# Expert routing of one transformer layer: the search for the eight highest logits moved into the LayerNorm stage, the weights onto GpSimd, and the ranks computed ahead of the totals

## The chip, the cores and the metric

One core of a Trainium2 chip runs the whole program. The metric is the device time of one execution in microseconds; the median of three runs of the kernel before is 1215.02 us. A core has five engines, each with its own queue of instructions: TensorE (PE in the profile; its weight loads are PEld), VectorE (DVE), ScalarE (ACT), GpSimd (POOL) and SyncE (SP), which here only starts transfers.

## What is computed

The input is 4 sequences of 512 rows of 512 numbers, 2048 rows in all, in 32-bit floats. The reference, cut to what matters:

```python
x = x + _layernorm(attention(_layernorm(x)))          # 16 heads, causal, rotary
x = x + _layernorm(ffn(_layernorm(x)))
# ffn, for all T = 2048 rows xt:
logits = xt @ router_w.T                              # 64 experts
top_w, top_i = jax.lax.top_k(softmax(logits), 8)
top_w = top_w / jnp.sum(top_w, axis=-1, keepdims=True)
# every row goes to its 8 experts, with these weights:
h_e = (silu(xt @ Wg[e].T) * (xt @ Wu[e].T)) @ Wd[e].T
# and one shared expert takes all rows, scaled by sigmoid(xt @ Wse.T)
```

As the weights are divided by their sum, the softmax over all 64 logits isn't needed in full: exp(logit - highest) of the eight chosen, divided by the sum of those eight, is the same.

## The kernel before

The rows are 16 tiles of 128. The work runs in stages: attention; then the LayerNorm stage; then routing together with the shared expert; then the routed experts, 128 gathered rows at a time; then the last sums and LayerNorm. The order on each engine is written out by hand: every engine's program is a list of operations with waits on semaphores, and an engine does them in that order.

**LayerNorm stage** (a loop over tiles on each engine, staggered). For tile i PE projects the attention's output into PSUM (`project`, L753). DVE takes its statistics (L1048, L1049), ACT the square root (L546), DVE the reciprocal (L1057) and the normalized row `delta` (L1058). POOL adds it to x (L397). In the next turn of the loop DVE takes the statistics of the sum (L1052, L1053), ACT the root (L550), DVE the reciprocal (L1063) and the normalized row `xn` (L1067). SP writes `xn` to memory (L312), for the gathers later, and PE turns it (`turn_x2`, L761); ACT takes it out of PSUM (L557), PE multiplies it by the router (`route`, L769), and ACT takes out 64 logits and the shared expert's one (L562). PE's order in a turn is `project(i)`, `route(i-3)`, `turn_x2(i-2)`.

**Routing**, on DVE unless it is said otherwise, begins when all 16 tiles have logits: the highest (L1072), ACT's Exp (L566), the softmax (L1085), the eight highest of each tile (L1087), their places (L1091, L1094), a running sum over tiles of who chose which expert (L1096, 16 in a chain), the weights (L1101 to L1104) and their transfer by SP (L315). PE counts the rows of each expert (`count_rows`, L814); DVE rounds the counts to tiles of 128 (L1111 to L1115). PE sums those over experts (L821, L822) and computes where each row stands within its expert (`place_rows`): for each half of the tiles, two products of 512 columns (L827, L828) and eight of 64 (L830), accumulated in one bank. DVE turns the places into slot numbers (L1129, then a max for each tile at L1136, then integers). PE's `tile_rows` (L835) and DVE's L1151 to L1158 make the list of which expert each block of 128 slots belongs to. Last, a table from slots to rows: 128 pairs of DVE operations (L1164, L1165) make one-hot matrices in a ring of eight, and PE multiplies each pair into the table (`fill_table`, L841, eight pairs to a tile).

**The shared expert** runs on PE, ACT and POOL at the same time, tile by tile: `shared_up` (L789), ACT's Silu and a copy (L575, L576), POOL's product (L404), `shared_turn` (L799), ACT (L580), `shared_down` (L805), ACT (L584). The routing's PE work is placed in this loop by hand: `count_rows` in the turn i = 3, `place_rows` and `tile_rows` in the turn i = 4, `fill_table(i - 6)` from the turn 6 on, and the last six tiles of it behind the loop. Behind its products POOL writes the shared rows to memory (L408, two transfers of 2 MB), and SP loads the weights of one more expert (L317).

**The routed stage** begins with DVE's L1169 to L1183 behind the last L841, the first gather by POOL (L414) and `turn_rows` (L870).

## Time and profile before

| what | us |
|---|---|
| median of 3 runs (1214.99 to 1217.04) | 1215.02 |
| the profiled execution's own time | 1215.08 |
| its span, from first to last instruction | 1213.2 |
| PE busy | 1055.3 (87%) |
| DVE busy | 702.6 (58%) |
| POOL busy | 628.7 (52%) |
| ACT busy | 469.4 (39%) |
| mean granted TensorE clock | 0.943 |

The times of the sections below are microseconds from the span's start in that one profiled execution. Its own time is 1.9 us over its span. "x8" behind an operation is the number of instructions merged into a row; a 32-bit product is two records. The bracket at the end of a row is the engine's idle time before it and what ended it. Ends of matmuls are modelled, and busy shares are means over a stretch.

### The profile page before, as it was taken

To read this page: it belongs to the slowest core of one execution; us is meant where nothing else is said; L and a number is where in the kernel's file an instruction comes from. 1 tells how busy PE (TensorE), PEld (TensorE's weight loads), DVE (VectorE), ACT (ScalarE), POOL (GpSimd) and SP (SyncE) were. 2 spreads that over 40 slices of the span, in tenths; PEclk is the share of its full clock that TensorE was granted. 3 is DMA by queue.
4 is the path that set the end of the run, shared out by engine and by line. 5 is a ranking of instruction groups with operands and counts; after the bars stand their busy time and mean duration, and the time that the engine had idled before them with its cause. 6 is when DMAs were issued, how large, how long until landed. Compare 5 with 4: busy or idle time off the path is not lost.

```text
span 1213.2 us, 24246 instructions
## 1 busy us (share of the span) xinstructions
PE 1055.3 (87%) x6243; PEld 717.2 (59%) x6244; DVE 702.6 (58%) x2355; ACT 469.4 (39%) x1354; POOL 628.7 (52%) x633
## 2 busy tenths in 40 slices
PE   5799899899999989878879999999999999999300
PEld 3455566555666545546447777777777777777200
DVE  3666566556666668758845544545444544454287
ACT  1666566556666732242212222222222222222122
POOL 4333333333333312200138888888888888788534
PEclk9899999989999999889969999999999999999755
DMA  9600000000000061100339999999999999997592
GB/s 353 230 2 1 4 1 2 3 2 2 1 2 2 1 234 52 61 18 1 115 117 210 221 212 256 227 240 239 264 228 256 230 255 265 253 201 136 118 386 98
DMA packets 65968, 166.80 MB, mean 137 GB/s; under 512 B 15570, under 2 KB 16850, under 8 KB 65760
## 3 DMA queue, kind: packets, MB, share of 16 engines
q0 software_dynamic: 38816, 83.95, 31.3%
q1 hardware_dynamic: 27072, 81.88, 19.2%
q8 instruction: 38, 0.62, 0.2%
q14 instruction: 42, 0.34, 0.1%
HBM read 121.03 MB, written 62.65 MB: 151 GB/s over the span
## 4 chain that ended last, share of the span: by engine, by line
PE 69%; DMA 11%; DVE 10%; issue 4%; ACT 2%; POOL 2%; DVEq 0%; POOLq 0%; SPq 0%; ACTq 0%
PE ps L886 16%; PE ps L638 14%; PE ps L897 8%; DMA sum_rows<-x_t,idx 6%; PE ps L697 6%; PE ps L753 4%; PE ps L870 4%; PE ps L667 4%; PE ps L717 4%; DMA x_t<-x_rows,idx 3%; PE ps L789 2%; PE ps L652 2%; POOL sum_rows L420 1%; PE ps L769 1%; PE ps L805 1%
## 5 line engine op out<-in xcount | busy, mean ns | idle before, releaser
L886 PE MATMUL ps<-big,work 128*128 x1264 | 300.8, 381 | 0.0
L420 POOL DMA_INDIRECT sum_rows<-x_t,idx x157 | 250.1, 1593 | 51.1 <-issue 41.1
L886 PEld LDWEIGHTS ps<-big,work 128*128 128x128 f32 x1264 | 229.0, 191 | 24.9
L414 POOL DMA_INDIRECT x_t<-x_rows,idx x163 | 170.5, 1046 | 71.5 <-issue 30.8
L638 PE MATMUL ps<-big 128*128 128x384 f32 x512 | 180.5, 496 | 1.5 <-ACT big L483 1.1
L359 POOL TENSOR_TENSOR work<-qkv_all,rope_sb 128x256 f32<-128x256 f32 x64 | 46.7, 730 | 251.6 <-ACT qkv_all L488 251.5
L594 ACT ACTIVATE work<-ps 128x512 f32<-128x512 f32 x159 | 95.0, 597 | 198.4 <-PE ps L870 147.9
L897 PE MATMUL ps<-big,work 128*128 x314 | 161.1, 594 | 0.9 <-issue 0.7
L870 PEld LDWEIGHTS ps<-ident_sb,x_t 128*128 128x128 f32 x636 | 79.0, 143 | 101.9 <-issue 75.9
L970 DVE CUSTOM_DVE_ANT_0 ps<-ps,mask_sb 128x128 f32<-128x128 f32 (+3 forms) x256 | 120.8, 512 | 24.0 <-PE ps L667 23.4
L505 ACT ACTIVATE work<-ps,neg_max 128x128 f32<-128x128 f32 (+3 forms) x256 | 132.4, 528 | 4.3 <-DVE neg_max L970 3.2
L638 PEld LDWEIGHTS ps<-big 128*128 128x128 f32 x512 | 94.5, 195 | 56.4 <-issue 3.7
L1198 DVE SCALAR_TENSOR_TENSOR work<-work,small,ps 128x128 f32<-128x128 f32 x157 | 54.5, 347 | 123.6 <-ACT work L599 92.5
L599 ACT ACTIVATE work<-ps 128x128 f32<-128x128 f32 x157 | 43.6, 278 | 196.3 <-PE ps L886 140.5
L697 PE MATMUL ps<-ident_sb,work 128*128 128x128 f32 x640 | 98.9, 285 | 18.2 <-ACT work L505 10.5
L511 ACT ACTIVATE x_t<-ps 128x128 f32<-128x128 f32 (+2 forms) x192 | 77.1, 436 | 91.7 <-PE ps L697 91.7
L870 PE MATMUL ps<-ident_sb,x_t 128*128 128x128 f32 x636 | 97.5, 276 | 14.3 <-DMA x_t<-x_rows,idx 12.5
L1206 DVE TENSOR_SCALAR x_t<-ps 128x512 f32<-128x512 f32 x157 | 106.9, 681 | 0.0
L697 PEld LDWEIGHTS ps<-ident_sb,work 128*128 128x128 f32 x640 | 69.0, 141 | 55.1 <-issue 44.4
L991 DVE TENSOR_TENSOR attn_t<-ps,work 128x128 f32 (+1 forms) x64 | 18.7, 292 | 112.3 <-PE ps L717 112.3
L1192 DVE TENSOR_SCALAR small<-x_t 128x1 f32 x158 | 24.3, 154 | 81.0 <-issue 77.3
L897 PEld LDWEIGHTS ps<-big,work 128*128 128x128 f32 x314 | 59.0, 190 | 11.4 <-issue 3.7
(166 smaller groups left out, 1419.4 us busy)
## 6 DMA issues: line engine op xcount, KB each, us to landing
big<-experts SPq DMA_DIRECT2D x65, 768.0 KB, 14.7
sum_rows<-x_t POOLq DMA_DIRECT2D x4, 2048.0 KB
big<-sum_rows SPq DMA_DIRECT2D x6, 1024.0 KB, 11.0
x_sb<-x SPq DMA_DIRECT2D x4, 1024.0 KB, 15.2
x_rows<-work SPq DMA_DIRECT2D x16, 256.0 KB, 2.0
sum_rows<-attn_t POOLq DMA_DIRECT2D x2, 2048.0 KB
out<-x_sb SPq DMA_DIRECT2D x16, 256.0 KB, 2.1
x_t<-sum_rows SPq DMA_DIRECT2D x3, 1024.0 KB, 14.5
```

The costliest lines, as they stand in the source:

```text
L414: pool.indirect_dma_start(rows[:, q, :], None, x2_rows, bass.IndirectOffsetOnAxis(ap=idx[:, q, 0:1], axis=0), bounds_check=last_row, oob_i ...
L420: pool.indirect_dma_start(sum_rows[p], bass.IndirectOffsetOnAxis(ap=idx[:, q, 1:2], axis=0), y_sb[:, q, :], None, bounds_check=last_row, o ...
L505: act.activation(probs[:, h, 0:n], s_bank[h][:, 0:n], ACT.Exp, bias=neg_max[:, h:h + 1], scale=-1.0, accum_out=den[:, h:h + 1]).then_inc(s ...
L511: act.activation(probs_t[:, i % 2, h, 0:qt + 1, :], pt_bank[h % 2].rearrange("p (k n) -> p k n", k=TB)[:, 0:qt + 1, :], ACT.Copy).then_inc ...
L594: act.activation(rows_t[:, p, :, :], ps[:, p, :].rearrange("p (c n) -> p c n", c=DC), ACT.Copy).then_inc(s_xg, 1)
L638: mm = pe.matmul(bank[:, 0:QKV], x_t[:, c, bass.ts(t, P)], wqkv_sb[:, c, g % G, :], start=(c == 0), stop=(c == DC - 1))
L697: mm = pe.transpose(pt_bank[h % 2][:, bass.ts(c, P)], probs[:, h, bass.ts(c, P)], ident_sb[:, :])
L870: mm = pe.transpose(ps[:, p, bass.ts(c, P)], rows[:, q, bass.ts(c, P)], ident_sb[:, :])
L886: mm = pe.matmul(ps[:, 2 + p, 0:GATEUP], rows_t[:, p, c, :], w_ring[:, slot, c * GATEUP:(c + 1) * GATEUP], start=(c == 0), stop=(c == DC - 1))
L897: pe.matmul(ps[:, 5 + p, :], hidden_t[:, p, :], w_ring[:, slot, DC * GATEUP:WCOLS], start=True, stop=True).then_inc(s_dn, 1)
L970: dve.tensor_tensor_reduce(sc, sc, mask_sb[:, S - n:S], -SCALE, 3.0e38, ALU.add, ALU.min, neg_max[:, h:h + 1]).then_inc(s_masked, 1)
L1206: dve.tensor_scalar(y_sb[:, q, :], ps[:, 5 + q % 2, :], 1.0, None, ALU.mult).then_inc(s_y, 1)
```

## The change

In the LayerNorm stage DVE does, for the tile whose logits are there (k = i - 4), a max of eight (`top`), a match_replace into `unchosen` and a comparison that gives `chosen`. `xn` is no longer computed by DVE: DVE makes -mean x 1/std in a small column, and ACT computes `xn` with it. POOL adds up `earlier` tile by tile behind L397, for the tile k = i - 4. ACT exponentiates the difference from the highest logit, for the eight highest and for all 64, in one operation each. POOL multiplies the weights by `chosen` and by 1/sum, between its products of the shared expert. On PE the two products of a half that need no totals (`spread_rows`) are done ahead of and behind `count_rows`, all in turn 0 of the shared loop, and the eight products of 64 columns of a half are one of 512. `tile_rows` moves to turn 2, `fill_table(i - 4)` begins in turn 4, and four tiles of it are left behind the loop.

```diff
+        unchosen = work[:, 384:512].rearrange("p (a e) -> p a e", a=2)
+        top_e = work[:, 512:512 + TILES * K].rearrange("p (t k) -> p t k", k=K)
...
@@ gpsimd
-            for i in range(TILES):
-                pool.wait_ge(s_stat, i + 1)
-                pool.tensor_tensor(out=x_sb[:, i, :], in0=x_sb[:, i, :], in1=delta[:, i % 2, :],
-                                   op=ALU.add).then_inc(s_x1, 1)
+            for i in range(TILES + 4):
+                if i < TILES:
+                    pool.wait_ge(s_stat, i + 1)
+                    pool.tensor_tensor(out=x_sb[:, i, :], in0=x_sb[:, i, :], in1=delta[:, i % 2, :],
+                                       op=ALU.add).then_inc(s_x1, 1)
...
+                if i >= 4:
+                    k = i - 4
+                    pool.wait_ge(s_chosen, k + 1)
...
+                    pool.tensor_tensor(out=earlier[:, k + 1, :], in0=earlier[:, k, :], in1=chosen[:, k, :],
+                                       op=ALU.add).then_inc(s_prefix, 1)
...
+                if i == 1:
+                    pool.wait_ge(s_e1, 1)
+                    pool.tensor_tensor(out=prob_e, in0=prob_e, in1=chosen, op=ALU.mult).then_inc(s_masked_e, 1)
+                if i == 3:
+                    pool.wait_ge(s_share, 1)
+                    pool.wait_ge(s_masked_e, 1)
+                    share = rt[:, 3, :].rearrange("p (t o) -> p t o", o=1).broadcast_to([P, TILES, E])
+                    pool.tensor_tensor(out=prob_e, in0=prob_e, in1=share, op=ALU.mult).then_inc(s_comb, 1)
@@ scalar
+                if 1 <= i <= TILES:
+                    r = i - 1
+                    act.wait_ge(s_nmr, r + 1)
+                    if r >= 2:
+                        act.wait_ge(s_x2d[r % 2], 16 * (r // 2))
+                        act.wait_ge(s_x2t_ps, r - 1)
+                    act.activation(xn[:, r % 2, :], x_sb[:, r, :], ACT.Identity, bias=small[:, r % 4, 7:8],
+                                   scale=small[:, r % 4, 6:7]).then_inc(s_x2, 1)
+
+            act.wait_ge(s_log, TILES)
+            act.activation(rt[:, 4, :], logits[:, :, E], ACT.Exp, scale=-1.0).then_inc(s_e2, 1)
             act.wait_ge(s_neg, 1)
-            for i in range(TILES):
-                act.activation(prob_e[:, i, :], logits[:, i, 0:E], ACT.Exp, bias=rt[:, 0, i:i + 1],
-                               accum_out=rt[:, 1, i:i + 1]).then_inc(s_e1, 1)
-            act.activation(rt[:, 4, :], logits[:, :, E], ACT.Exp, scale=-1.0).then_inc(s_e1, 1)
+            act.activation(top_e, top_e, ACT.Exp).then_inc(s_e2, 1)
+            act.wait_ge(s_neg, 2)
+            act.activation(prob_e, prob_e, ACT.Exp).then_inc(s_e1, 1)
@@ tensor
+            def spread_rows(half):
...
+                pe.wait_ge(s_prefix, 8 * half + 8)
...
+                pe.matmul(o, before_sb[:, :], mine, start=True, stop=False)
+                pe.matmul(o, ones_sb[:, :], ahead, start=False, stop=False)
...
-                    pe.matmul(o, before_sb[:, :], mine, start=True, stop=False)
-                    pe.matmul(o, ones_sb[:, :], ahead, start=False, stop=False)
-                    for k in range(8):
-                        mm = pe.matmul(o[:, k * E:(k + 1) * E], n_rep, below_sb[:, :], start=False, stop=(k == 7))
-                mm.then_inc(s_slots_ps, 1)
+                    below_8 = below_sb[:, :].rearrange("f (o e) -> f o e", o=1).broadcast_to([E, 8, E])
+                    pe.matmul(ps[:, half, :], n_rep, below_8, start=False, stop=True).then_inc(s_slots_ps, 1)
...
-                if i == 4:
+                if i == 0:
+                    spread_rows(0)
+                    count_rows()
+                    spread_rows(1)
                     place_rows()
                 if i >= 1:
                     shared_turn(i - 1)
-                if i == 4:
+                if i == 2:
                     tile_rows()
                 if i >= 1:
                     shared_down(i - 1)
-                if i == 3:
-                    count_rows()
-                if i >= 6 and i < TILES:
-                    fill_table(i - 6)
-            for n in range(TILES - 6, TILES):
+                if i >= 4 and i < TILES:
+                    fill_table(i - 4)
+            for n in range(TILES - 4, TILES):
                 fill_table(n)
@@ vector, LayerNorm stage
+            for i in range(TILES + 4):
+                y_in, x_in, l_in = i < TILES, 1 <= i <= TILES, i >= 4
+                r, k = i - 1, i - 4
...
+                if l_in:
+                    dve.wait_ge(s_log, k + 1)
+                    tops = mark(dve.max(top[:, k, :], logits[:, k, 0:E]))
...
+                if l_in:
+                    dve.wait_ge(s_own, tops)
+                    left = mark(dve.match_replace(unchosen[:, k % 2, :], top[:, k, :], logits[:, k, 0:E], MASKED))
...
+                if l_in:
+                    dve.wait_ge(s_own, left)
+                    dve.tensor_scalar(chosen[:, k, :], unchosen[:, k % 2, :], MASKED, None, ALU.is_equal).then_inc(s_chosen, 1)
...
-                    dve.tensor_scalar(xn[:, r % 2, :], x_sb[:, r, :], small_x[:, 4:5], small_x[:, 6:7],
-                                      ALU.subtract, ALU.mult).then_inc(s_x2, 1)
-            dve.wait_ge(s_log, TILES)
...
+                    dve.scalar_tensor_tensor(out=small_x[:, 7:8], in0=small_x[:, 4:5], scalar=-1.0, in1=small_x[:, 6:7],
+                                             op0=ALU.mult, op1=ALU.mult).then_inc(s_nmr, 1)
+
+            def highest(n):
+                return top[:, :, 0:1].broadcast_to([P, TILES, n])
+
+            dve.tensor_tensor(out=top_e, in0=top[:, :, :], in1=highest(K), op=ALU.subtract).then_inc(s_neg, 1)
+            dve.tensor_tensor(out=prob_e, in0=logits[:, :, 0:E], in1=highest(E), op=ALU.subtract).then_inc(s_neg, 1)
```

Left out here: L1072 to L1104 are removed from DVE; behind L1115 it takes the sum of the eight exponentials and the two reciprocals (of that sum and for the sigmoid); and L1129 waits for each half by itself.

## Rows read from the trace of the kernel before

**Rows 1.** Busy us (count) by engine and stretch, PEclk, DMA share, GB/s:

```profile
450.00:470.00 20.00, 20.00 (x84) 11.70 (x83) 16.40 (x37) 5.65 (x19) 5.10 (x5) 1.00 0.20 75
...
510.00:517.00 7.00, 5.63 (x24) 4.73 (x24) 0.89 (x4) 2.08 (x7) 0.00 (x0) 0.50 0.20 75
...
540.00:560.00 20.00, 18.22 (x88) 11.99 (x88) 12.24 (x64) 3.57 (x10) 0.93 (x2) 1.00 0.12 28
```

**Rows 2.** Timeline, one LayerNorm tile: start us, us, engine, line, operation [idle before]:

```profile
495.57 0.70 DVE L1048 BATCH_NORM_STATS2 stats<-ps 128x6 f32<-128x512 f32 x1 [0.47 <-PE ps L753]
...
497.37 0.81 DVE L1058 TENSOR_SCALAR work<-ps,small 128x512 f32<-128x512 f32 x1
...
498.26 1.26 POOL L397 TENSOR_TENSOR x_sb<-x_sb,work 128x512 f32<-128x512 f32 x1 [3.45 <-DVE work L1058]
...
498.29 1.52 DVE L1067 TENSOR_SCALAR work<-x_sb,small 128x512 f32<-128x512 f32 x1
...
500.29 0.70 DVE L1048 BATCH_NORM_STATS2 stats<-ps 128x6 f32<-128x512 f32 x1 [0.47 <-PE ps L753]
...
500.81 0.48 PEld L761 LDWEIGHTS ps<-ident_sb,work 128*128 128x128 f32 x4
```

**Rows 3.** Lines L1067, L617, L1237, L468: ns minimum/median/maximum, first and last start:

```profile
L1067 DVE TENSOR_SCALAR work<-x_sb,small x16: 546/1522/1525, 442.7 to 510.6; 128x512 f32<-128x512 f32 x16
...
L617 ACT ACTIVATE big<-big,moments,rstd x8: 799/801/814, 1166.4 to 1181.3; 128x512 f32<-128x512 f32 x8
...
L1237 DVE TENSOR_TENSOR big<-big x8: 683/686/1752, 1156.3 to 1171.0; 128x512 f32<-128x512 f32 x8
...
L468 POOL TENSOR_TENSOR x_sb<-x_sb,big x8: 1515/1707/1708, 1167.3 to 1184.9; 128x512 f32<-128x512 f32 x8
```

**Rows 4.** Timeline, start and end of the LayerNorm stage on PE:

```profile
444.27 0.66 PE L761 MATMUL ps<-ident_sb,work 128*128 128x128 f32 x4 [0.90 <-DVE work L1067]
...
516.39 5.19 PE L789 MATMUL ps<-big,x_t 128*128 128x256 f32 x16
...
526.23 0.46 PE L799 MATMUL ps<-ident_sb,work 128*128 128x128 f32 x1 [4.65 <-POOL work L404]
```

**Rows 5.** Timeline, the stretch of the ranks:

```profile
539.29 0.14 DVE L1111 COPY n_col<-ps 64x1 f32<-64x1 f32 x1
...
540.59 0.24 PE L821 MATMUL ps<-n_col,upto_sb 64*64 64x1 f32 x2 [1.87 <-DVE qkv_all L1115]
...
540.96 1.12 PE L827 MATMUL ps<-qkv_all,before_sb 128*128 128x512 f32 x2
...
542.88 2.00 PE L830 MATMUL ps<-below_sb,qkv_all 64*128 64x64 f32 x16
...
548.90 0.48 PE L835 MATMUL ps<-qkv_all,ones_sb 64*1 64x192 f32 x2
```

**Rows 6.** Timeline of DVE, slots and first pairs:

```profile
550.07 2.12 DVE L1136 MAX8 work<-wo_sb 128x8 f32<-128x64 f32 x16
...
554.47 0.24 DVE L1164 TENSOR_SCALAR low<-count_h,work 128x128 f16<-128x128 f16 x1
...
554.87 0.23 DVE L1164 TENSOR_SCALAR low<-count_h,work 128x128 f16<-128x128 f16 x1
```

**Rows 7.** Timeline, groups of L841 and their end:

```profile
553.86 1.89 PE L789 MATMUL ps<-big,x_t 128*128 128x256 f32 x8
...
557.41 0.94 PE L841 MATMUL ps<-high,low 128*128 128x192 f16 x8
...
595.75 0.82 PE L841 MATMUL ps<-high,low 128*128 128x192 f16 x8
...
616.10 0.36 DVE L1169 COPY qkv_all<-ps 128x192 f32<-128x192 f32 x1 [0.43 <-PE ps L841]
```

**Rows 8.** A stretch of two us behind the loop, and the first gather:

```profile
610.00:612.00 2.00, 1.69 (x6) 0.52 (x5) 2.00 (x12) 0.00 (x0) 0.00 (x0) 0.50 0.10 39
...
618.67 1.09 POOL L414 DMA_INDIRECT x_t<-x_rows,idx  x1 [18.57 <-DVE idx L1183]
```

## What the change will do: the prediction

> **What bounds the kernel now.** The profiled execution takes 1215.08 us (span 1213.2), 0.06 over the 1215.02 median of the runs, so its sums hold for the median as well. A measurement of this kernel can tell about 0.2% (2.4 us) from no change. The diff touches only 433 to 618 us; I read the busy time of that stretch first, then its timeline tile by tile.
>
> In the LayerNorm stage PE is busy 20.00 of 20 us, and a tile takes 4.72 us from one L1048 to the next [rows 1, 2]. DVE is busy 16.40 of 20, so it has room. The search for the eight highest begins on all tiles at once, behind the last logits, which leave PE about when L789 starts (516.39). PE still does L789 for two tiles and then has nothing: L799 at 526.23 had 4.65 us of idle time ahead of it [rows 4]. The ranks then hold PE's queue from L821 at 540.59 to L835 behind the last L830 at 548.90, 8.3 us [rows 5], and only at 554.47 does DVE begin the 128 pairs of L1164 and L1165 [rows 6]. Their matmuls (L841, eight to a tile) start at 557.41 and are issued once per tile of the shared expert, every (595.75 - 557.41)/9 = 4.26 us: PE bound. The six groups left over at 595.75 go at DVE's pace, 0.40 us a pair, and end at 616.10 [rows 6, 7]. That end releases the first gather at 618.67, and everything behind it is the routed stage, which the change doesn't touch. So the path that counts is: LayerNorm tiles, ranks, ten groups at PE's pace, six at DVE's. What moves 616.10 moves the end.
>
> **LayerNorm stage.** Removed from DVE: L1067, 1.52 us at the median though 0.55 when nothing is in its way [rows 3]. It starts 0.03 us after POOL's L397 (498.29 against 498.26) and is held by it: its end, 1.55 after POOL's start, less its own 0.55 gives a release 1.00 us after POOL's start [rows 2, 3]. ACT does this work instead, in the form of L617, 0.80 us [rows 3]. DVE gains a max, a match_replace, an is_equal and a one-column product. The max of 16 tiles ends within 2.12 us, 0.13 each [rows 6]; match_replace and is_equal on 64 columns have no row here that I use, so between nothing and L1048's 0.70 each; I take 0.2, near the small max. DVE drops in sum, so it hides them. What counts is where they stand: between L1048 and L1058 they add about 0.15 (max and match_replace mostly run while DVE would wait for its own statistics), and by as much L1058 and POOL's L397 start later.
>
> The new product (into small column 7) stands where L1067 stood, 0.03 us behind the start of L397, and reads two SBUF operands. Nearest rows: L1237, two SBUF operands, takes 0.68 alone and 1.75 beside POOL [rows 3]; L1067 is held 0.98. Bounds: held not at all, or for POOL's whole 1.27. I take 1.00, then 0.16 of its own, 0.06 to hand over and 0.80 on ACT: the normalized row is there 2.02 us after POOL's start, where L1067 had it at 1.55. The Trainium skill (SBUF — State Buffer, Who interferes with whom) says that a Vector instruction with two SBUF inputs contends with a GpSimd one that reads SBUF and that the second to issue fully blocks. By that rule the forecast's own sum stands; a reader who thinks only of L1067's mode would leave it out. L1237 agrees that such a form suffers, but POOL's operation suffers with it there (1.71 against 1.27), so the block isn't one-sided [rows 2, 3].
>
> In the steady tile the row is then ready at 2.69 + 0.15 + 2.02 = 4.86 us after L1048's start, and PE's L761 wants it at 500.81 - 495.57 = 5.24 [rows 2]. It stays hidden with 0.4 to spare: period unchanged. The waits that L1067 had for its buffer (the row's transfer by SP, two tiles old, and L761) are ACT's now, and behind them in ACT's queue stands the square root of the next tile; the row ends at 4.86 and that root isn't due before the next L1048 at 4.72 plus its 0.70, so nothing is late. It isn't hidden at the two ends. At the start L761 waited for L1067 (0.90 us, at 444.27) [rows 4]: +0.47. In the tail, where PE has no L753 left to do, it is waited for as well: +0.47 again and +0.15 for the later L397. Stage end: +1.1, so L789 at 517.5 and the last logits half a us behind it, about 517.9. POOL's prefix adds (64 columns, between nothing and L397's 1.27; I take 0.3) follow L397 and lie in its idle time; the last one, behind the last chosen, is done by about 519.2.
>
> **Search and weights.** Off the path: sixteen max and match_replace, 16 chained L1096, 16 Exp with accumulator reads. Left behind the last logits: one tile's max, match_replace, is_equal (0.6), two subtractions, an Exp of 1024 columns. ACT's Silu then starts about 523, and the first L799 could go at about 524. DVE's column chain from L1111 to L821, 1.30 us [rows 5], starts behind the count at about 523 and ends at 524.2, before PE needs it. The two weight products go to POOL, 1024 columns each, so twice L397: 2.5 us. They hold a DVE operation each (slot integers, then a pair), and delay no product of the shared expert, as POOL has idle time between them (in 540 to 560 it was busy 0.93 of 20 us) [rows 1]. SP's transfer of the weights waits for the second product, and behind it in SP's queue stands only the load that waits for the last shared tile.
>
> **Ranks on PE.** PE's queue is now L789 of tile 0 (slow clock: 16 took 5.19, eight at full clock 1.89, so 3.3; from 517.5 to 520.8 [rows 4, 7]), ranks of half 0 (540.96 to 542.88: 1.92), count 0.2, ranks of half 1 1.92, the two small products 0.37, and the offsets. These were 16 records in 2.00 us a half, mostly fixed cost; now one 512-column product a half, as L827, so 1.92/2 each, 1.92 for both. Bounds: 1.0 and the old 4.0. Sum: 520.8 + 1.92 + 0.2 + 1.92 + 0.37 + 1.92 = 527.1, where L789 of tile 1 starts [rows 5].
>
> **Fill.** A shared tile without a group takes 557.41 - 553.86 = 3.55 [rows 7]. Group 0 stands behind tile 4's instead of tile 6's: 527.1 + 4 x 3.55 = 541.3. Is DVE there by then? Before, the sixteen max of the slots began at 550.07 and the first pair at 554.47, 4.4 us later. Now the slots of half 0 are taken while PE does half 1, the others from 527.2, so the max begin about 528 and the first pair could go at 532.4. POOL's first weight product holds the slot integers for about 2 us: 534.4. The row table (L835, which runs while PE waits for ACT in tile 2's turn, about 533) is in time for that. Eight pairs take 8 x 0.40, and POOL's second product holds one of them for up to 2.5: 534.4 + 3.2 + 2.5 = 540.1, in time by 1.2 [rows 5, 6]. Twelve groups go inside the loop: 541.3 + 11 x 4.26 = 588.2. From the last of them to the end was 20.35 us for six groups; with two fewer, 16 x 0.40 = 6.4 less: 13.95. End: 602.1, against 616.10 [rows 6, 7]. **Gain 14.0 us**: 1215.08 - 14.0 = 1201.1.
>
> **What is late next.** The shared rows' two 2 MB writes and one expert's load fill the DMA engines up to 610 (share 0.10 in 610 to 612) [rows 8]. They hang on the loop's end, which moves by 588.2 - 595.75 = -7.5, so to about 602.7; the first gather comes at 618.67 - 14.0 = 604.7 [rows 8]. Clear by 2 us.
>
> **Rivals.**
> A. The column product isn't held. Then the row is ready at 1.05 after POOL's start, the stage ends about 0.5 us earlier instead of 1.1 later: 1199.5. For it: it touches 128 values only. Against: it stands 0.03 us behind POOL's start as L1067 does. The blocking rule cited above is what this case denies. 17%.
> B. The normalized row becomes the LayerNorm stage's bound. One turn and four pairs of L753 later it frees two tiles' PE work, so each us past 5.24 costs half a us per tile. Were POOL slowed as in L468 (+0.44) and DVE's new operations double (+0.7), the row comes at 6.0: 0.38 a tile over 13 tiles, +5: 1206. For: the spare is 0.4. Against: every term had its row. 11%.
> C. The DMA burst isn't clear of the gathers: it costs up to 2 us, as the same bytes end at 602.7 at best: 1203. 6%.
> D. Slower: TensorE's clock stays at 1.2 GHz (granted 0.50 from 510 to 517 [rows 1]) behind the denser rank work. L789 costs 1.4 more a tile, L805 and L841 about as much together, so about 3 us a tile; from five tiles on it eats the 14 us, and for all sixteen it is 1215 + 34 = 1249. For: the change puts its rank work right behind that slow stretch. Against: before, the clock had come back under the same L789 by the time of the ranks, and the shared tiles ran at 1.00 (540 to 560) [rows 1]. 3%.
> The forecast itself: 63%.
>
> **Numbers.** 1201.1. Low end: A, and a clock back before the end of the first L789 (another 1.5 us): 1197. High end: B: 1206.5. Faster over 0.2%: all but D and a heap of small misses, 95%; within 0.2% 2%; slower 3%.
>
> **What would show it.** First L761 about 0.5 us later; the period still 4.72; the column product near 1.1 us; no PE gap between 518 and 530; L841's first at about 541 and its last at about 601.7; first gather at 604.7. Wrong if the period is over 4.8, if PE waits for DVE at the first groups of L841, or if the last four groups aren't at 0.40 a pair.

## The result, and the profile after

The changed kernel takes 1201.05 us (median of 4 runs, 1199.17 to 1202.32) against 1215.51 us of the kernel before beside it (4 runs): ratio 0.9882, 95% interval 0.9862 to 0.9901. That is 14.5 us less; 1201.1 was predicted. The profiled execution took 1200.51 us, its span 1198.6. Busy time by engine:

```profile
PE 1045.2 (87%) x6215; PEld 711.7 (59%) x6216; DVE 694.8 (58%) x2349; ACT 478.0 (40%) x1340; POOL 636.7 (53%) x652
```

Two stretches of the part where PE had waited for the search, and two behind the loop (busy us by engine, PEclk, DMA share, GB/s). PE, which had nothing to do for 4.65 us [rows 4], is now busy 6.00 of 6 us from 520 to 526, and its clock stays at the upper level:

```profile
520.00:526.00 6.00, 6.00 (x21) 2.90 (x21) 4.23 (x20) 0.19 (x2) 0.45 (x1) 1.00 0.01 3
526.00:532.00 6.00, 5.22 (x21) 3.02 (x20) 5.76 (x24) 1.92 (x7) 3.22 (x3) 1.00 0.00 0
598.00:600.00 2.00, 1.45 (x5) 0.42 (x4) 1.56 (x8) 0.00 (x0) 0.00 (x0) 0.50 0.99 406
600.00:602.00 2.00, 0.00 (x0) 0.00 (x0) 0.90 (x6) 0.00 (x0) 0.00 (x0) 0.50 0.14 55
```

One tile of the LayerNorm stage, in the timeline (start us, us, engine, line, operation), which answers to [rows 2]. L1121 is the new one-column product, L596 the row on ACT, L797 the turn on PE:

```profile
493.60 0.70 DVE L1090 BATCH_NORM_STATS2 stats<-ps 128x6 f32<-128x512 f32 x1 [0.69 <-PE ps L789]
...
496.34 1.27 POOL L405 TENSOR_TENSOR x_sb<-x_sb,work 128x512 f32<-128x512 f32 x1 [3.17 <-DVE work L1115]
496.37 1.26 DVE L1121 SCALAR_TENSOR_TENSOR small<-small 128x1 f32<-128x1 f32 x1
...
497.66 0.81 ACT L596 ACTIVATE work<-x_sb,small 128x512 f32<-128x512 f32 x1 [1.36 <-DVE small L1121]
...
498.32 0.70 DVE L1090 BATCH_NORM_STATS2 stats<-ps 128x6 f32<-128x512 f32 x1 [0.70 <-PE ps L789]
498.85 0.48 PEld L797 LDWEIGHTS ps<-ident_sb,work 128*128 128x128 f32 x4
```

The period is still 4.72 us (493.60 to 498.32). L1121 starts 0.03 us behind POOL's sum and lasts 1.26; the row is ready at 498.47, 4.87 us into the tile, and PE wants it at 5.25. At the stage's start PE waits for it longer than before, 1.48 us against 0.90 [rows 4]:

```profile
442.30 0.66 PE L797 MATMUL ps<-ident_sb,work 128*128 128x128 f32 x4 [1.48 <-ACT work L596]
```

The ranks on PE's queue, which answer to [rows 4, 5]: one product of 512 columns a half (L872) ends what had been 32 records.

```profile
514.58 3.72 PE L825 MATMUL ps<-big,x_t 128*128 128x256 f32 x8
...
518.10 1.46 PE L855 MATMUL ps<-qkv_all,before_sb 128*128 128x512 f32 x2
...
522.87 1.98 PE L872 MATMUL ps<-below_sb,qkv_all 64*128 64x512 f32 x4
...
524.78 1.99 PE L825 MATMUL ps<-big,x_t 128*128 128x256 f32 x8
```

DVE and POOL up to the first group of L882, against [rows 6, 7]. POOL's two weight products (L427, L432) hold one DVE operation each, 2.41 and 1.95 us; still, DVE has its eight pairs ready early and waits for PE at 539.39:

```profile
527.74 2.36 POOL L427 TENSOR_TENSOR wo_sb<-wo_sb,qkv_all 128x1024 f32<-128x1024 f32 x1
527.77 2.41 DVE L1169 TENSOR_SCALAR slot_i<-work 128x128 int32<-128x128 f32 x1
...
534.91 1.90 POOL L432 TENSOR_TENSOR wo_sb<-wo_sb,rt 128x1024 f32<-128x1024 f32 x1
534.91 1.95 DVE L1195 TENSOR_SCALAR high<-count_h,work,token_sb 128x192 f16<-128x192 f16 x1
...
539.11 0.82 PE L882 MATMUL ps<-high,low 128*128 128x192 f16 x8
...
539.39 0.25 DVE L1194 TENSOR_SCALAR low<-count_h,work 128x128 f16<-128x128 f16 x1 [2.13 <-PE ps L882]
```

And the end of the fill, against [rows 7, 8]:

```profile
585.82 0.82 PE L882 MATMUL ps<-high,low 128*128 128x192 f16 x8
...
602.31 1.09 POOL L441 DMA_INDIRECT x_t<-x_rows,idx  x1 [12.13 <-DVE idx L1213]
```

Taken from the same places in both traces, and counted from the first projection of the LayerNorm stage (432.8 before, 430.3 after), this is where the time went:

| us from the first projection | before | after |
|---|---|---|
| shared expert's tile 0 on PE | 83.6 | 84.3 |
| first pair on DVE | 121.7 | 101.8 |
| first group of pairs on PE | 124.6 | 108.8 |
| table copied out, behind the last pair | 183.3 | 169.5 |
| first gather issued | 185.9 | 172.0 |
| first gathered rows turned on PE | 189.6 | 175.7 |

The gain inside the changed stretch is 13.8 us. The two untouched parts differ between these two executions: the attention ended 2.5 us earlier, the part from the first gather on took 596.3 instead of 594.5. In all profiles of this study the first projection starts between 429.9 and 433.5, and the part from the first gather on takes 592.6 to 597.2 us (run 10 apart), so differences of a microsecond or two in the whole time are read below from the stretch itself, not from the median.

The stretch has a variation of its own. Near the end of the LayerNorm stage TensorE's granted clock falls from 1.00 to 0.50 in every profile, but not at the same place: about 76.5 us from the first projection in the kernel before and in runs 5 to 9, about 78.5 in the changed kernel and in runs 1 to 4 and 10 to 12. Run 9 leaves this stage and the ranks as they are in the changed kernel, so the two show what the place is worth. Here are the changed kernel (first projection at 430.26) and run 9 (432.63), each with PE's busy us, PEclk, DMA share and GB/s where the clock falls, and the turn of tile 14:

```profile
508.00:509.00 1.00, 0.62 (x4) 0.86 0.23 86
...
507.96 0.65 PE L797 MATMUL ps<-ident_sb,work 128*128 128x128 f32 x4 [1.19 <-ACT work L596]
```

```profile
509.00:510.00 1.00, 0.15 (x2) 0.56 0.00 0
...
510.33 1.12 PE L798 MATMUL ps<-ident_sb,work 128*128 128x128 f32 x4 [1.18 <-ACT work L597]
```

Where the clock falls early, the same turn takes 1.12 us instead of 0.65 and tile 0 starts at 84.8 instead of 84.3; the clock is also back earlier (86.7 instead of 88.7), so tile 1 starts at 93.8 instead of 94.5 and the last copy at 168.6 instead of 169.5. What decides the place is not shown. Runs are therefore compared below with a run whose clock fell at the same place, wherever less than 1 us is at stake.

### The profile page after: what moved, and what is told of

The parts are those of the page before. It is cut to its first block, busy times and chain, and to the rows that moved or that the text cites. A ratio compares the mean times of both kernels' runs of the same rounds, so it can differ in the third digit from the quotient of the medians.

```text
span 1198.6 us, 24208 instructions
## 1 busy us (share of the span) xinstructions
PE 1045.2 (87%) x6215; PEld 711.7 (59%) x6216; DVE 694.8 (58%) x2349; ACT 478.0 (40%) x1340; POOL 636.7 (53%) x652
## 4 chain that ended last, share of the span: by engine, by line
PE 68%; DMA 14%; DVE 8%; issue 4%; POOL 2%; ACT 2%; DVEq 0%; POOLq 0%; SPq 0%; ACTq 0%
PE ps L928 14%; PE ps L674 14%; DMA sum_rows<-x_t,idx 8%; PE ps L939 7%; PE ps L733 6%; DMA x_t<-x_rows,idx 5%; PE ps L789 4%; PE ps L703 4%; PE ps L912 4%; PE ps L753 4%; PE ps L825 3%; PE ps L688 2%; POOL sum_rows L447 1%; PE ps L841 1%; PE ps L805 1%
## 5 line engine op out<-in xcount | busy, mean ns | idle before, releaser
L733 PE MATMUL ps<-ident_sb,work 128*128 128x128 f32 x640 | 98.7, 285 | 17.2 <-ACT work L532 10.5
## 6 DMA issues: line engine op xcount, KB each, us to landing
x_t<-sum_rows SPq DMA_DIRECT2D x3, 1024.0 KB, 14.5
```

Source lines behind the costliest of these rows:

```text
L733: mm = pe.transpose(pt_bank[h % 2][:, bass.ts(c, P)], probs[:, h, bass.ts(c, P)], ident_sb[:, :])
```

## The experiments

All are edits of the changed kernel unless it is said otherwise, each executed 4 to 12 times. The kernel before took 1215.32 us beside runs 1, 2, 3 and 5, 1214.88 beside runs 6 to 9 and 1214.62 beside runs 4 and 10 to 12, against 1215.51 beside the changed kernel, so medians of different groups can be 0.9 us apart for this alone; each ratio is to the kernel before of its own group. Places "from the first projection" are those of the table above.

**1. Groups from turn 6.**

```diff
-                if i >= 4 and i < TILES:
-                    fill_table(i - 4)
-            for n in range(TILES - 4, TILES):
+                if i >= 6 and i < TILES:
+                    fill_table(i - 6)
+            for n in range(TILES - 6, TILES):
```

> The changed kernel, but the groups of L841's matmuls begin in turn 6 of the shared loop as before, and six are left behind it. My theory, that the end of the stage is tiles of the shared expert at PE's pace and the rest at DVE's 0.40 us a pair: first group 2 x 3.56 = 7.1 us later than in the changed kernel (539.1 to 546.2), ten groups at 4.25, then 20.3 us as before instead of 13.9, so the last pair ends 5.0 us later and the run takes 1206 us. Rival, the shared rows' transfers or something else gates the first gather: within 1 us of the changed kernel's 1201.

Measured 1205.58 us, ratio 0.9922 (0.9909 to 0.9936). Counted from the first projection, the first group comes at 115.9 instead of 108.8 (+7.1), the last copy at 174.5 instead of 169.5 (+5.0). Both are the numbers expected; the rival is out.

**2. The ranks in turn 4 as well.**

```diff
                 if i == 0:
-                    spread_rows(0)
                     count_rows()
+                if i == 4:
+                    spread_rows(0)
                     spread_rows(1)
                     place_rows()
...
-                if i == 2:
+                if i == 4:
                     tile_rows()
```

> The same as the run with groups from turn 6, and besides the rank products, the offsets and the expert row go back from turns 0 and 2 to turn 4 (the count stays in turn 0). My theory: PE's work is the same and DVE is still ready before turn 6, so where the ranks stand is worth nothing by itself, only the turn in which the groups can begin: within 1 us of that run, about 1206 to 1207. Rival, the early ranks are a gain of their own, since they fill PE's gap behind the first tile: 3 us or more above that run.

Measured 1204.91 us, 0.9908 (0.9894 to 0.9922), not to be told from run 1; the last copy is at 174.4, against 174.5 there. The early ranks have no gain of their own. They are what lets the groups begin in turn 4, and that is worth 5 us.

**3. Eight offsets a half.**

```diff
-                    below_8 = below_sb[:, :].rearrange("f (o e) -> f o e", o=1).broadcast_to([E, 8, E])
-                    pe.matmul(ps[:, half, :], n_rep, below_8, start=False, stop=True).then_inc(s_slots_ps, 1)
+                    o = ps[:, half, :]
+                    for k in range(8):
+                        mm = pe.matmul(o[:, k * E:(k + 1) * E], n_rep, below_sb[:, :], start=False, stop=(k == 7))
+                    mm.then_inc(s_slots_ps, 1)
```

> The changed kernel, but the offsets of a half are eight products of 64 columns again instead of one of 512. My theory: PE holds the path there, so the whole difference is in the end: two halves of 1.92 to 2.0 against about 1.0 each, +2.0 us, 1203. Rival, they are hidden behind DVE's slot work or the waits for ACT: within 0.5 us of the changed kernel.

Measured 1207.56 us, 0.9932 (0.9918 to 0.9946): three times my +2.0, and a miss. The timeline, and the clock behind the 32 records (busy us of PE, PEclk, DMA share, GB/s):

```profile
526.04 4.47 PE L873 MATMUL ps<-below_sb,qkv_all 64*128 64x64 f32 x32
...
530.44 3.78 PE L825 MATMUL ps<-big,x_t 128*128 128x256 f32 x8
```

```profile
526.00:528.00 2.00, 2.00 (x20) 1.00 0.04 8
528.00:530.00 2.00, 2.00 (x16) 0.74 0.00 0
530.00:538.00 8.00, 7.51 (x17) 0.50 0.00 0
538.00:540.00 2.00, 2.00 (x8) 0.70 0.00 0
540.00:542.00 2.00, 1.82 (x7) 1.00 0.01 4
```

The records take 4.40 us (526.04 to 530.44) against 1.91 for L872. PE was never idle in them, and yet the granted clock falls to 0.50, its 1.2 GHz level, from about 529 to 539. The shared tile behind them takes 3.78 us instead of 1.99, the next 3.08, and the first group comes 6.3 us later (115.2 against 108.8 from the first projection). In the kernel before, the same 32 records stood between shared tiles and the clock stayed at 1.00 [rows 1]. But they weren't in a row there: behind the 16 of half 0 [rows 5] came the rank products of half 1, four records of 512 columns, and then the 16 of half 1:

```profile
544.80 1.12 PE L827 MATMUL ps<-qkv_all,before_sb 128*128 128x512 f32 x2
...
546.72 2.00 PE L830 MATMUL ps<-below_sb,qkv_all 64*128 64x64 f32 x16
```

Here all the rank products stand ahead, and the 32 narrow records follow each other for 4.40 us.

**4. Eight offsets a half, with the ranks in turn 4** (runs 2 and 3 together).

> The run with the ranks in turn 4 and, besides, the offsets as eight products of 64 columns. In turn 0 the eight cost 6 us and not 2, since the granted clock fell to 0.50 for about 10 us behind them; in the kernel before the same 32 records, in turn 4, left it at 1.00. Theory, it is the place (directly behind the slow stretch and the rank products of turn 0): here +2 us over the run with ranks in turn 4, 1207, clock 1.00. Rival, the fall comes with the 32 narrow records wherever they stand in this kernel: +6 us, 1211, clock 0.50 behind them.

Measured 1208.60 us, 0.9962 (0.9945 to 0.9979). PE in two-microsecond stretches:

```profile
538.00:540.00 2.00, 2.00 (x21) 1.00 0.00 0
540.00:542.00 2.00, 2.00 (x8) 0.71 0.00 0
542.00:544.00 2.00, 2.00 (x5) 0.50 0.00 0
544.00:546.00 2.00, 1.48 (x7) 0.94 0.01 4
```

The clock falls here too, but for some 3.5 us instead of 10; the last copy comes 3.3 us after that of run 2 (177.7 against 174.4). So the place matters, as the theory had it, but the fall isn't bound to turn 0: neither expectation is met. Why the kernel before was spared stays open. That its narrow records stood in two sets of 16 with 1.92 us of wide products between them, while runs 3 and 4 have all 32 in a row, is a rival that neither expectation names and no run tests.

**5. Weights on DVE.** The two products are taken from POOL, and DVE does the first in its wait for the count (L1123) and the second behind the reciprocals (L1145).

```diff
-                if i == 1:
-                    pool.wait_ge(s_e1, 1)
-                    pool.tensor_tensor(out=prob_e, in0=prob_e, in1=chosen, op=ALU.mult).then_inc(s_masked_e, 1)
...
+            dve.wait_ge(s_e1, 1)
+            dve.tensor_tensor(out=prob_e, in0=prob_e, in1=chosen, op=ALU.mult).then_inc(s_masked_e, 1)
...
+            dve.wait_ge(s_share, 1)
+            dve.wait_ge(s_masked_e, 1)
+            dve.tensor_tensor(out=prob_e, in0=prob_e, in1=share, op=ALU.mult).then_inc(s_comb, 1)
```

> The changed kernel, but both weight products are on DVE (the first in its wait for the count, the second behind the reciprocals) instead of on POOL, where they hold a DVE operation each for 2.4 and 1.9 us. My theory: the first pair begins about 1 us earlier and the eighth about 2.5 us earlier, but PE's first group doesn't, as it stood behind PE's own tiles (DVE waited 2.1 us for it): no change, within 0.5 us of 1201. Rival, the holds are on the path: 1.5 to 2.5 us faster.

Measured 1201.19 us, 0.989 (0.9873 to 0.9908): no change. DVE's timeline:

```profile
533.48 0.07 DVE L1178 MEMSET col_i<- 1x12 int32 x1 [1.91 <-PE ps L868]
...
541.89 0.25 DVE L1194 TENSOR_SCALAR low<-count_h,work 128x128 f16<-128x128 f16 x1 [3.41 <-PE ps L874]
```

DVE is ready earlier and waits longer: 1.91 us for the expert row (L1178) and 3.41 us for the first group to be used, against 2.13 in the changed kernel. The last copy stands at 168.8 against 169.5, and that 0.7 us comes from the clock, which fell and came back 2 us earlier here: the shared expert's products of tile 0 took 2.95 us and 3.72 (L825) in the changed kernel. Against run 9, whose clock fell at the same place and which has the products on POOL, nothing is left: tile 1 starts at 93.8 in both, the last copy at 168.8 here and 168.6 there. The weights cost nothing on either engine.

**6. The one-column product with one tensor input.**

```diff
-                    dve.scalar_tensor_tensor(out=small_x[:, 7:8], in0=small_x[:, 4:5], scalar=-1.0, in1=small_x[:, 6:7],
-                                             op0=ALU.mult, op1=ALU.mult).then_inc(s_nmr, 1)
+                    dve.tensor_scalar(small_x[:, 7:8], small_x[:, 4:5], small_x[:, 6:7], -1.0,
+                                      ALU.mult, ALU.mult).then_inc(s_nmr, 1)
```

> The changed kernel, but the one-column product of DVE (mean x -1 x 1/std) is a tensor_scalar whose second factor is a per-partition scalar, so it has one SBUF tensor input instead of two. In the changed kernel it lasts 1.25 us beside POOL's sum against 0.16 alone. Theory, it is held for its second tensor input: now 0.15 to 0.2 us, PE's first turned tile 1.1 us earlier, the stage about 1.3 us shorter, 1199.7. Rival, any small DVE operation with an SBUF output of this kind (a tensor_scalar in a fast mode, as the slot integers that lasted 2.41 us) is held: unchanged 1.25, 1201.

Measured 1199.53 us, 0.9877 (0.9858 to 0.9896). The product in the changed kernel, then in this one (ns minimum/median/maximum, first and last start):

```profile
L1121 DVE SCALAR_TENSOR_TENSOR small<-small x16: 160/1256/1258, 440.1 to 508.6; 128x1 f32<-128x1 f32 x16
```

```profile
L1121 DVE TENSOR_SCALAR small<-small x16: 214/214/215, 442.4 to 510.0; 128x1 f32<-128x1 f32 x16
```

It isn't held any more: the mechanism is as expected. PE's first turn comes at 11.0 us instead of 12.0. For the rest the comparison is with runs 5 and 9, whose clock fell at the same place: tile 0 starts at 83.1 instead of 84.8, 1.7 us earlier, but tile 1 at 92.9 instead of 93.8 and the last copy at 167.9 instead of 168.6 to 168.8. So 0.7 to 0.9 us arrive, not the 1.3 expected. The clock is back at the same place in all three (86.7 to 86.8), so the 1.7 us are spent on tile 0 at 0.50, where its products take 3.3 us for 1.89 at 1.00 [rows 4, 7]: by these rows an estimated 1.0 us. The medians are 1.5 us apart, with overlapping intervals.

**7. The product ahead of delta.** The reciprocal and the one-column product stand before L1115, so POOL's sum hasn't started; no line is changed, only moved.

```diff
+                if x_in:
+                    dve.wait_ge(s_std_x, r + 1)
+                    dve.wait_ge(s_var_x, r + 1)
+                    step(dve.reciprocal(small_x[:, 6:7], small_x[:, 6:7]))
...
                 if y_in:
                     dve.wait_ge(s_own, y_scale)
```

> The changed kernel, but the reciprocal and the one-column product for the row stand ahead of the normalized row delta (L1115) on DVE, so POOL's sum isn't running yet. Theory: the product lasts 0.16 us; delta and POOL's sum come 0.6 us later; the first turned tile comes 1.4 us earlier (PE's own work then stands first), the tail about 0.3 us later because the last statistics wait for POOL: net 1.1 us faster, 1200. Rival, delta is what paces the stage: the period goes from 4.72 to over 5, 5 us or more slower.

Measured 1199.71 us, 0.9883 (0.9866 to 0.9899); the same two-input operation:

```profile
L1117 DVE SCALAR_TENSOR_TENSOR small<-small x16: 159/160/160, 441.4 to 510.4; 128x1 f32<-128x1 f32 x16
```

With the form kept and only its place changed, it lasts 0.16 us: it is POOL's sum that holds it. The first turn comes at 10.5, 1.5 us earlier, and the period stays 4.72. Of this little arrives: against runs 9 and 5, tile 0 starts at 84.0 for 84.8, tile 1 at 93.4 for 93.8, and the last copy is at 168.4 for 168.6 and 168.8. The 1.1 us expected aren't there.

**8. The kernel before, with the row on ACT alone** (L1067 replaced by the one-column product, and the row made by ACT as in the changed kernel).

```diff
-                    dve.tensor_scalar(xn[:, r % 2, :], x_sb[:, r, :], small_x[:, 4:5], small_x[:, 6:7],
-                                      ALU.subtract, ALU.mult).then_inc(s_x2, 1)
+                    dve.scalar_tensor_tensor(out=small_x[:, 7:8], in0=small_x[:, 4:5], scalar=-1.0, in1=small_x[:, 6:7],
+                                             op0=ALU.mult, op1=ALU.mult).then_inc(s_nmr, 1)
```

> The kernel before with one part of the change alone: the normalized row xn is made by ACT from DVE's one-column product (no search in the LayerNorm stage, nothing else). My theory: a cost, not a gain: +0.5 us at the stage's start, as much in its tail, period unchanged at 4.72: 1215.5 + 1 = 1216.5. Rival, moving it off DVE shortens the stage: 1 to 3 us faster.

Measured 1217.09 us, 1.0018 (1.0005 to 1.003): 2.2 us over the kernel before beside it, where 1.0 was expected. Its product:

```profile
L1073 DVE SCALAR_TENSOR_TENSOR small<-small x16: 160/1258/1261, 442.4 to 510.7; 128x1 f32<-128x1 f32 x16
```

Stage end 84.7 against 83.6, last copy 184.3 against 183.3, with the clock falling at the same place: +1.0 to 1.1 in the stretch, as expected. The rest of the median's 2.2 isn't in it.

**9. Shared rows written early.** Twelve tiles are written in POOL's turn 13, four behind the loop.

```diff
+                if i == 13:
+                    pool.wait_ge(s_sy, 12)
+                    pool.dma_start(sums_v[0][:, 0:12, :], y_shared[:, 0:12, :]).then_inc(s_scatter[0], 16)
...
-            for half in range(2):
-                pool.wait_ge(s_sy, 8 * half + 8)
-                pool.dma_start(sums_v[0][:, 8 * half:8 * half + 8, :],
-                               y_shared[:, 8 * half:8 * half + 8, :]).then_inc(s_scatter[0], 16)
+            pool.wait_ge(s_sy, TILES)
+            pool.dma_start(sums_v[0][:, 12:TILES, :], y_shared[:, 12:TILES, :]).then_inc(s_scatter[0], 16)
```

> The changed kernel, but POOL writes the shared rows of tiles 0 to 11 (3 MB) in turn 13 and only the last four tiles (1 MB) behind the loop, instead of two writes of 2 MB behind it. In the changed kernel the writes keep the DMA engines full until about 600, and the first gather is issued at 602.3. My theory, they are just clear of the gathers: no change, within 0.7 us of 1201, with the DMA engines idle from about 594. Rival, they delay the first gathers or the first scatters: 1 to 3 us faster.

Measured 1200.98 us, 0.9896 (0.9879 to 0.9914): no change, with the DMA engines free from 596 on (share 0.02). The columns are those of the stretches above:

```profile
592.00:596.00 4.00, 2.89 (x10) 0.97 (x10) 4.00 (x21) 0.00 (x0) 0.00 (x0) 0.81 0.97 398
596.00:600.00 4.00, 3.42 (x10) 1.05 (x10) 4.00 (x21) 0.00 (x0) 0.00 (x0) 0.50 0.02 7
```

**10. Even fill.** Five pairs between turn and down, where PE waits for ACT, and five behind down, from turn 3 on.

```diff
-                if i >= 4 and i < TILES:
-                    fill_table(i - 4)
-            for n in range(TILES - 4, TILES):
-                fill_table(n)
+                if i >= 3:
+                    fill_pairs(5)
...
+                if i >= 3:
+                    fill_pairs(5)
+            fill_pairs(TILES * K)
```

> The changed kernel, but the pairs' matmuls are spread evenly: from turn 3 on five between turn and down of the shared tile (where PE waits 0.59 us for ACT) and five behind down, instead of eight once a turn from turn 4 and 32 behind the loop. If the stage's end is set by DVE's pace and its stalls alone, DVE now runs through: 128 x 0.40 plus the holds, 57 us from the first pair, so the last pair ends 10 us earlier than in the changed kernel (about 590) and the run takes 1191. Rival, the shared rows' two writes become the bound, as they still begin behind the loop (now about 590) and last 13 us: the first gathered rows can't land before about 603, so at most 3 us faster, 1198.

Measured 1201.36 us, 0.9891 (0.9875 to 0.9906). The last copy comes at 158.9, 10.6 us earlier than in the changed kernel, as expected of a stage paced by DVE, and the time is that of the changed kernel:

```profile
596.73 1.09 POOL L441 DMA_INDIRECT x_t<-x_rows,idx  x1 [1.58 <-issue]
...
607.98 1.97 PE L917 MATMUL ps<-ident_sb,x_t 128*128 128x128 f32 x8 [14.76 <-DMA x_t<-x_rows,idx]
```

```profile
592.00:594.00 2.00, 1.12 (x2) 0.30 (x2) 0.52 (x3) 0.73 (x2) 0.00 (x0) 1.00 1.02 387
602.00:604.00 2.00, 0.00 (x0) 0.00 (x0) 0.00 (x0) 0.00 (x0) 1.58 (x2) 0.50 1.04 424
604.00:608.00 4.00, 0.02 (x1) 0.02 (x1) 0.00 (x0) 0.00 (x0) 0.43 (x1) 0.50 1.02 361
```

The first gather is issued at 596.73 and its rows reach PE at 607.98; in between the DMA engines are full, with the shared rows' writes ahead of the gathers. Counted from the first projection the rows reach PE at 175.4, in the changed kernel at 175.7. The rival decides, and for more than I gave it: it takes everything. A part of that is that the writes themselves come later: the loop's turns now carry ten pairs, and the first write is issued at 157.8 instead of 154.9.

**11. Even fill with the early shared rows** (edits 9 and 10 together).

> Even fill and, besides, the shared rows of tiles 0 to 11 are written in turn 13 and only 1 MB behind the loop. If the writes are what holds even fill back (the rival of that run), this one gets the whole gain: 1191 to 1192. If they are not, it equals even fill.

Measured 1194.34 us, 0.9844 (0.9823 to 0.9865). The last copy is at 159.2, as in run 10, and now worth 6.7 us against the changed kernel: the first rows reach PE at 169.7, 6.0 us earlier. So the writes were what held it. Not the whole 10: the engines are still at 0.95 in 596 to 600, with the last 1 MB, the expert's load and the gathers themselves:

```profile
596.00:600.00 4.00, 0.00 (x0) 0.00 (x0) 0.00 (x0) 0.00 (x0) 3.09 (x4) 0.50 0.95 326
```

**12. All three** (edits 6, 9 and 10).

> Even fill, early shared rows, and the one-column product with one SBUF tensor input. The product's 1.2 to 1.5 us lie in the LayerNorm stage, ahead of everything else, so they should add up: 1.3 us below the run with even fill and early rows, about 1190. Rival, PE or the transfers take them back: equal to it.

Measured 1192.96 us, 0.9838 (0.9821 to 0.9855): faster than both kernels of this study, by 21.7 us and 8.1 us. The product's part shows in the stage end (83.5 against 84.3 in run 11, clock alike), but of these 0.9 us 0.5 are left at the last copy (158.7 against 159.2) and 0.2 at the first rows on PE. The 1.4 us between the medians of runs 11 and 12 are inside their intervals, so the 1.3 expected are not shown.

## Why the prediction was right, point by point

**The size.** 14.0 us was forecast and 14.5 measured by the medians; in the stretch it is 13.8, or 14.5 to 14.7 where the clock falls at the same place as in the kernel before (runs 5 and 9, last copy at 168.8 and 168.6 against 183.3). The untouched parts (2.5 us less, 1.8 more) happened nearly to cancel in the profiled execution, which is luck, not foresight: runs 1 to 12 show that they move by this much on their own. Two bounds of the range don't follow from its sums: 1199.5 less 1.5 is 1198.0, not 1197, and rival B's price gives 1206.1, not 1206.5.

**LayerNorm stage.** Forecast +1.1, measured +0.7 in the profiled execution, but its clock fell 2 us later than that of the kernel before; with the clock alike it is +1.2 (run 9, 84.8 against 83.6), and +1.1 where the row is moved alone (run 8). The hold of the new product, chosen from L1067's row (1.00 us), is 1.10 (1.26 against 0.16): it ends 0.02 us behind POOL's sum (497.63 against 497.61), so it waits for the whole of it. The row was forecast ready 4.86 us into a tile and was at 4.87, but by two small errors that cancel: POOL's sum starts 2.74 us into the tile for 2.84, and the row is there 2.13 us behind that start for 2.02. The period didn't move. By the rule cited from the Trainium skill (SBUF — State Buffer, Who interferes with whom) the product would be held for its second SBUF input: runs 6 and 7 agree, 1.26 us with two inputs beside POOL's sum, 0.21 with one, 0.16 with two but ahead of it. POOL's sum itself stays at 1.27 beside a product of one column, where L468 had taken 1.71 in a stretch with L1237's long additions [rows 3].

**Rival A** (not held) is refuted for the change as it was made, but its price at the stage's end was right: forecast 1.6 us, from 1.1 late to 0.5 early, and run 6 measures 1.7, with the end 0.5 us ahead of the kernel before. The step from there to the time was wrong: only 0.7 to 0.9 of it arrives at the last copy, as PE spends it at the lower clock. **Rival B** (the row becomes the bound) stayed away by the 0.4 us that the sum left.

**Ranks on PE.** From tile 0 to tile 1, 9.6 us were forecast and 10.2 came: the clock returned later, and the first rank product still ran partly slow (518.10, 1.46 us). In runs 5 and 9 it is 9.0. Counted from the first projection tile 1 was forecast at 94.3 and starts at 94.5, in those runs at 93.8: stage end and ranks err in opposite directions. The two offset products took 1.91 for 1.92.

**DVE in time.** First pair 7.3 us behind the start of tile 1, exactly as forecast; the first group 14.3 against 14.2; DVE ahead of PE (forecast 1.2 us, by its wait more like 2). Runs 5 and 9 show that POOL's holds cost nothing.

**The fill.** Twelve groups in (585.82 - 539.11)/11 = 4.25 us each, then 13.91 us to the copy for a forecast 13.95. Run 1 gives the step's worth by itself, run 2 shows that the ranks' place has none but through it. With the narrow offsets put back as well (run 4), the last copy is still at 177.7 against 183.3 in the kernel before, although the groups begin in turn 6 in both. So of the 13.8 us, 5.6 belong to what run 4 keeps, which is above all the search moved ahead (the row on ACT, in it too, costs 1.0 by run 8), 3.3 to the wide offsets (run 4 to run 2) and 5.0 to the two groups, the first of them to within the 0.9 us that the clock's place makes. No run has the search alone.

**What is late next.** The writes were forecast clear of the first gather by 2 us; they end near 600.3 and it is issued at 602.31. Runs 9 and 10 show both sides: nothing gained when they go, everything lost when the fill ends 10.6 us sooner. Rival C was rightly small here, and would have been the whole story with 10 us more.

**Where a step was wrong.** I bounded the offsets by "1.0 and the old 4.0", as if the old form's price were its records' time. In its new place it costs 6.3 us, as TensorE's clock goes down behind it (run 3). Rival D was built on such a fall but put it behind the dense rank work; that work left the clock at 1.00 in the changed kernel, and with the narrow products in place of the wide ones it fell, in two places (runs 3 and 4). What about them does it isn't shown, as the kernel before had them too, in two sets of 16, and kept its clock. The forecast stood because it needed only the new form. The single product of 512 columns, which I counted as 2 us, is therefore worth about 6 in this arrangement.

## What to carry to other kernels

Find the loop in which two engines hand each other work, and count how much of that work is done inside it and how much is left behind it: here each tile's group moved into the loop was worth 2.5 us, and the earlier ranks counted only because they let two more in. The earlier search had a worth of its own. Before moving an end forward, look at which transfers start at the same place; here an end that moved 10.6 us forward, into a burst of 13 us, gained nothing until most of the burst was moved too. An operation of one column can last eight times its own length beside another engine's (1.26 us for 0.16), and its form or its place in the queue removes that; what arrives at the end has to be measured there: of 1.0 and 1.5 us at PE's first turn, 0.7 to 0.9 and 0.2 to 0.4 did. And before a difference of under 1 us is read from two traces, see whether TensorE's clock changed at the same place in both.

## What the runs showed of the hardware that was not expected

A TensorE whose records show it busy can lose its clock. In run 3 it was busy 2.00 of each 2 us with 32 records of 64 columns and 64 rows in a row, and the granted clock went from 1.00 to 0.50 (2.4 to 1.2 GHz) for about 10 us; in run 4 the same records were followed by 3.5 us of it; the same offsets as four records of 512 columns left it at 1.00, and so did the 32 in two sets of 16 in the kernel before. Two executions with the same LayerNorm stage can lose the clock 2 us apart (78.5 and 76.5 us from the first projection), which moves the end of the stretch by 0.7 to 0.9 us. A DVE operation of one column with one tensor input isn't held by POOL (0.21 us), while one of 128 columns with one tensor input is (L1169, 2.41 us beside L427's 2.36). They differ in more than their size, as L1169 turns f32 into int32, and no run separates the two.
